# All down products of the first expert layer in three rounded passes, W2's split ahead of the layer, and the next layer's weights loaded into the place of their low parts

## The reference: what is computed

```python
x = x + cross_attention(layernorm(x), ctx)          # 16 heads of 8, 154 keys, masked
x = x + experts_0(layernorm(x))                     # 8 experts, 512 wide, top 2
x = x + second_attention(layernorm(x), ctx)         # causal, then cross, then a small feed-forward
x = x + experts_1(layernorm(x))                     # 32 experts, 64 wide, top 6 of 4 groups, a shared one
# experts_0:
h = gelu(einsum('td,edh->eth', xf, W1) + b1[:, None, :])
expert_out = einsum('eth,ehd->etd', h, W2) + b2[:, None, :]
out = einsum('etd,te->td', expert_out, weights)
```

## Time and profile before

| | us |
|---|---|
| median of three executions | 574.48 |
| lowest, highest | 572.86, 574.75 |
| profiled execution, its own time | 574.52 |
| its span, first to last instruction | 572.7 |
| PE busy | 556.3 (97%) |
| DVE busy | 447.4 (78%) |
| ACT busy | 376.1 (66%) |
| POOL busy | 170.1 (30%) |

### The profile page before, as it was taken

The page is one execution under the profiler, slowest core; times in us unless marked ns, Lnnn a source line. Parts: engine busy times, 40 slices in busy tenths (PEclk is TensorE's granted clock), DMA queues, the critical chain, the costliest instruction groups (busy, mean ns, idle before and its releaser), DMA issues.

```text
span 572.7 us, 8759 instructions
## 1 busy us (share of the span) xinstructions
PE 556.3 (97%) x2677; PEld 393.5 (69%) x2677; DVE 447.4 (78%) x1343; ACT 376.1 (66%) x663; POOL 170.1 (30%) x173
## 2 busy tenths in 40 slices
PE   7898999999999999999999999999999999999996
PEld 7565566665777667767677667677776766677885
DVE  6988999792555656877868787988988999879794
ACT  2576677768766787856976589873765532475553
POOL 4101120011242212163113324137012031455574
PEclk9999999999999999999999999999999999999998
DMA  4401000401111110111101111341221231432540
GB/s 137 186 19 29 1 9 2 148 1 38 56 38 38 38 47 19 38 38 40 69 31 37 58 36 38 106 147 57 92 92 68 99 98 64 146 110 84 158 146 24
DMA packets 23328, 38.42 MB, mean 67 GB/s; under 512 B 3792, under 2 KB 9552, under 8 KB 22896
## 3 DMA queue, kind: packets, MB, share of 16 engines
q1 hardware_dynamic: 22848, 37.44, 20.1%
q10 hardware_dynamic: 432, 0.40, 0.2%
HBM read 36.45 MB, written 1.38 MB: 66 GB/s over the span
## 4 chain that ended last, share of the span: by engine, by line
PE 86%; DVE 6%; ACT 3%; issue 2%; POOL 1%; DMA 1%; POOLq 0%; SPq 0%; ACTq 0%; DVEq 0%
PE ps L1640 11%; PE ps L1642 10%; PE ps L1641 10%; PE ps L1863 8%; PE ps L2036 5%; PE ps L1652 4%; PE ps L1739 4%; PE ps L1653 3%; PE ps L1654 3%; PE ps L1759 3%; PE ps L1635 3%; PE ps L1647 2%; PE ps L1773 2%; PE ps L1776 2%; PE ps L1940 2%
## 5 line engine op out<-in xcount | busy, mean ns | idle before, releaser
L1640 PE MATMUL ps<-xThi,w1s 128*128 128x512 f32 x256 | 122.5, 479 | 1.3 <-DVE h L1591 0.6
L999 ACT ACTIVATE h<-ps,early 128x512 f32<-128x512 f32 x128 | 86.1, 686 | 47.5 <-PE ps L1642 25.1
L1642 PE MATMUL ps<-xTlo,w1s 128*128 128x512 f32 x256 | 100.8, 394 | 0.0
L1641 PE MATMUL ps<-xThi,w1s 128*128 128x512 f32 x256 | 100.5, 393 | 0.0
L1130 ACT ACTIVATE s<-ps 128x512 f32<-128x512 f32 x68 | 40.7, 598 | 62.8 <-PE ps L1642 62.3
L862 POOL TENSOR_TENSOR acc_o<-acc_o,ty 128x512 f32<-128x512 f32 x32 | 43.6, 1361 | 85.1 <-DVE ty L1391 80.0
L1640 PEld LDWEIGHTS ps<-xThi,w1s 128*128 128x128 f32 x256 | 48.2, 188 | 26.3 <-issue 7.8
L1863 PE MATMUL ps<-h,w2s 128*128 128x512 f32 x128 | 65.8, 596 | 0.3 <-DVE ty L1391 0.3
L1295 DVE TENSOR_REDUCE NM<-ps 128x2 f32<-128x308 f32 x128 | 55.9, 471 | 5.5 <-PE ps L1739 3.8
L1352 DVE TENSOR_TENSOR h_r<-h,s_r 128x512 fp32r<-128x512 f32 x64 | 48.1, 752 | 14.7 <-ACT s_r L885 14.5
L1591 DVE TENSOR_TENSOR h<-s,ps 128x512 f32<-128x512 f32 x68 | 46.4, 682 | 15.7 <-PE ps L1642 12.0
(11 more groups left out here) (293 smaller groups left out, 1156.0 us busy)
## 6 DMA issues: line engine op xcount, KB each, us to landing
CB<-ct_rows SPq DMA_DIRECT2D x128, 128.0 KB, 2.9
WB<-wt_rows SPq DMA_DIRECT2D x32, 256.0 KB, 3.3
w2s<-w_dram SPq DMA_DIRECT2D x2, 2048.0 KB, 9.3
raw<-gu_dram SPq DMA_DIRECT2D x4, 512.0 KB, 4.1
x_in<-x_dram SPq DMA_DIRECT2D x4, 256.0 KB, 3.0
w2s<-dn_dram SPq DMA_DIRECT2D x1, 1024.0 KB, 4.7
out_dram<-ty SPq DMA_DIRECT2D x3, 256.0 KB, 3.0
late<-late_dram SPq DMA_DIRECT2D x1, 608.5 KB, 7.8
```

The costliest lines, as they stand in the source:

```text
L999: nc.scalar.activation(h32[:, c % HR, :], bank[c % 2], ACT.Gelu, bias=b1T[:, c:c + 1]).then_inc(b_gelu.sem, 1)
L1640: M(dst, w[0], xThi[:, x, :], start=start, stop=False)
L1641: M(dst, w[1], xThi[:, x, :], start=False, stop=False)
L1642: return M(dst, w[0], xTlo[:, x, :], start=False, stop=stop)
```

## The change

- `second`: every chunk's down product is `down3`; the f32 product of L1863 is gone.
- `highs_b` and `lows_b` run over all 32 chunks of a block instead of 16. The rounded copies rotate over three buffers (s32 and its twin hh0 have three slots instead of two) and no longer wait in pairs.
- `split2` has four pieces instead of two, contiguous ones; w2h holds all 4096 columns.
- The buffer raw1 is gone. A piece of the second layer's weights is loaded into the place of its low part (w1f and shf, the f32 twins of w1s and shs), and SP waits for PE's last reading of W1 there (`b_h_ps`) before the DMA. ACT then copies the high part, with no wait on PE, and POOL subtracts in place.
- All five tables of order are written anew.

```diff
-    w1s = sb("w1s", [P, 2, NC0 * P], F32R)
+    w1f, w1s = twins("w1s", [P, 2, NC0 * P])
-    w2h = sb("w2h", [P, NP1 * P], F32R)
-    odd, odd_low = (w.rearrange("p (c two k) -> p c two k", two=2, k=P)[:, :, 1, :] for w in (w2s[:], w2r[:]))
+    w2h = sb("w2h", [P, NC0 * P], F32R)
-    shs = sb("shs", [P, 2, 2 * P], F32R)
+    shf, shs = twins("shs", [P, 2, 2 * P])
-    s32, hh0 = twins("s32", [P, 2, S])
+    s32, hh0 = twins("s32", [P, 3, S])
+    HH = s32.shape[1]
-    raw1 = sb("raw1", [P, 2, 1024])
@@ SP, second_weights
-            for k, (src, w, _, _) in enumerate(pieces1):
-                yield
-                if not k:
-                    sp.wait_ge(a_x1.sem, a_x1.at(NB - 1, 1))
+            for k, (src, raw, _, _) in enumerate(pieces1):
+                yield
+                if k:
+                    sp.wait_ge(b_h_ps.sem, b_h_ps.at(NB - 1, 8 * k))
                 if k >= 2:
-                    sp.wait_ge(gu_lo.sem, k - 1)
-                sp.dma_start(raw1[:, k % 2, 0:w], src).then_inc(gu_loaded[k % 2].sem, 16)
+                    sp.wait_ge(gu_hi.sem, k - 1)
+                sp.dma_start(raw, src).then_inc(gu_loaded[k % 2].sem, 16)
@@ ACT, split1
-                if k:
-                    act.wait_ge(b_h_ps.sem, b_h_ps.at(NB - 1, 8 * k))
-                copy(dst[:, 0, c:c + w], raw1[:, k % 2, 0:w]).then_inc(gu_hi.sem, 1)
+                copy(hi, raw).then_inc(gu_hi.sem, 1)
@@ ACT, split2
-            for k in range(2):
+            for k in range(NDOWN):
                 yield
                 act.wait_ge(down0_loaded.sem, 16)
                 c = slice(1024 * k, 1024 * k + 1024)
-                copy(w2h[:, c].rearrange("p (c k) -> p c k", k=P), odd[:, 8 * k:8 * k + 8, :]).then_inc(w2_hi.sem, 1)
+                copy(w2h[:, c], w2s[:, c]).then_inc(w2_hi.sem, 1)
@@ ACT, highs_b
-            for j in range(NC0 // 2):
-                yield
-                act.wait_ge(b_gelu.sem, b_gelu.at(b, 2 * j + 2))
-                if b or j >= 2:
-                    act.wait_ge(b_y.sem, b_y.at(b, 2 * j - 2))
-                copy(hh0[:, j % 2, :], h32[:, (2 * j + 1) % HR, :]).then_inc(b_hi.sem, 1)
+            for c in range(NC0):
+                yield
+                act.wait_ge(b_gelu.sem, b_gelu.at(b, c + 1))
+                if b * NC0 + c >= HH:
+                    act.wait_ge(b_y.sem, b_y.at(b, c - HH + 1))
+                copy(hh0[:, (b * NC0 + c) % HH, :], h32[:, c % HR, :]).then_inc(b_hi.sem, 1)
@@ DVE, lows_b
-            for j in range(NC0 // 2):
+            for c in range(NC0):
                 yield
-                dve.wait_ge(b_hi.sem, b_hi.at(b, j + 1))
-                o = (2 * j + 1) % HR
-                V.tensor_tensor(h32r[:, o, :], h32[:, o, :], hh0[:, j % 2, :].bitcast(F32), ALU.subtract).then_inc(b_lo.sem, 1)
+                dve.wait_ge(b_hi.sem, b_hi.at(b, c + 1))
+                o = c % HR
+                V.tensor_tensor(h32r[:, o, :], h32[:, o, :], hh0[:, (b * NC0 + c) % HH, :].bitcast(F32), ALU.subtract).then_inc(b_lo.sem, 1)
@@ PE, second
-                j, at, ends = c // 2, c % 4 == 0, c % 4 == 3
-                if c % 2:
-                    pe.wait_ge(b_lo.sem, b_lo.at(b, j + 1))
-                    if b == 0 and j % 8 == 0:
-                        pe.wait_ge(w2_lo.sem, w2_lo.at(0, j // 8 + 1))
-                    w = w2h[:, j * P:(j + 1) * P], odd_low[:, j, :]
-                    down3(bank[2], w, (hh0[:, j % 2, :], h32r[:, c % HR, :]), at, ends).then_inc(b_y.sem, 1)
-                else:
-                    pe.wait_ge(b_gelu.sem, b_gelu.at(b, c + 1))
-                    M(bank[2], w2s[:, c * P:(c + 1) * P], h32[:, c % HR, :], start=at, stop=ends).then_inc(b_y.sem, 1)
+                at, ends, k = c % 4 == 0, c % 4 == 3, slice(c * P, (c + 1) * P)
+                pe.wait_ge(b_lo.sem, b_lo.at(b, c + 1))
+                if b == 0 and c % 8 == 0:
+                    pe.wait_ge(w2_lo.sem, w2_lo.at(0, c // 8 + 1))
+                down3(bank[2], (w2h[:, k], w2r[:, k]), (hh0[:, (b * NC0 + c) % HH, :], h32r[:, c % HR, :]), at, ends).then_inc(b_y.sem, 1)
...
 PLAN_ACT = {
-    "split2": [[12505, 14718]],
+    "split2": [[11383, 11522, 12013, 12100]],
```

More of the change, by code:

```diff
@@ L136 @@
[L136 to L144, removed]
@@ new lines @@
+    "halves_b": [[11478, 11945], [16472, 17004], [19960, 22069], [26317, 27260]],
+    "routing": [[11610, 11632, 11672, 12497, 12518, 12540, 12562, 12582], [16506, 16575, 17063, 17253, 18212, 18284,
+        18306, 18326], [20985, 21007, 21186, 21370, 22317, 22877, 22947, 23557], [27995, 28150, 28603, 28717, 29548,
+        30311, 30333, 30353]],
+    "stage_b": [[14234, 14884, 15491, 16181, 16712, 17271, 17910, 18393, 18674], [19495, 20444, 21127, 22003, 22758,
+        23679, 24236, 24767, 25050], [25934, 26578, 27725, 28619, 29256, 30000, 30593, 31402, 31771], [32308, 33559,
+        34237, 35274, 35869, 37028, 37737, 38183, 38650]],
@@ L310 @@
-    "prepare_b": [[10641, 11519, 12824], [15687, 17325, 18503], [19336, 21013, 23741], [27123, 27562, 31110]],
-    "first": [[12729, 13169, 13459, 13620, 13688, 13850, 13918, 14214, 14282, 14509, 14732, 14801, 15028, 15096, 15320,
[8 rows of a table removed]
-    "weights": [[13311], [19016], [25875], [32779]],
-    "second": [[13534, 13990, 14059, 14145, 14354, 14440, 14578, 14664, 14873, 14959, 15165, 15251, 15460, 15730,
[8 rows of a table removed]
-    "stage_c": [[16103, 17503, 19260, 19380, 19633, 19719], [25964, 26040, 26224, 26310], [32364, 32733, 32868, 32954]
-        , [38731, 39465, 39738, 39893]],
@@ L341 @@
[L341 to L342 removed]
[8 rows of a table removed]
[L351 removed]
[4 rows of a table removed]
+    "idle_turns": [[88, 156, 200, 245, 290, 335, 380, 424, 469, 514, 559, 604, 648, 688, 1138, 1213, 1236, 1258, 1333,
+        1356, 1442, 1740, 1980, 2097]],
@@ new lines @@
+    "context_keys": [[779], [1564], [4695], [7880]],
+    "context_values": [[720], [4263], [7264], [10126]],
+    "inputs": [[899, 1037], [2309, 2792], [5147, 5809], [8307, 8442]],
+    "queries": [[1387, 1683, 1891, 3090], [3811, 4743, 4987, 5991], [6826, 7710, 8073, 8914], [9498, 10530, 10805,
+        11675]],
+    "keys": [[1170, 1290], [3569, 3629], [6600, 6723], [9022, 10211]],
+    "maxima": [[1526, 1547, 1620, 1658, 1727, 1763, 1828, 1866], [1941, 1958, 2049, 2075, 2147, 2215, 2353, 2415],
[7 rows of a table added]
@@ new lines @@
+    "prepare_b": [[10687, 11178, 12884], [15543, 15796, 18370], [19031, 20303, 23632], [26163, 27025, 30576]],
+    "first": [[12767, 13230, 13505, 13582, 13673, 14008, 14077, 14307, 14447, 14516, 14722, 14860, 14929, 15141, 15334,
[8 rows of a table added]
+    "weights": [[13371], [18802], [25545], [32365]],
+    "second": [[13802, 13871, 13939, 14146, 14379, 14585, 14654, 14791, 15003, 15072, 15265, 15403, 15659, 15727,
[8 rows of a table added]
+    "stage_c": [[15222, 16229, 18657, 19212, 19397, 20712], [25400, 25634, 25818, 25904], [32229, 32307, 32454, 32541]
+        , [38345, 39278, 39465, 39731]],
@@ L657, in build_program @@
     NPIECE, NHALF = 4, 8
-    pieces1 = [(a["sh"][:, 0:2 * P], 2 * P, shs, 0)]
-    pieces1 += [(a["gu"][:, 1024 * k:1024 * k + 1024], 1024, gus, 1024 * k) for k in range(NPIECE)]
+    pieces1 = [(a["sh"][:, 0:2 * P], shf[:, 1, :], shs[:, 0, :], shs[:, 1, :])]
+    for k in range(NPIECE):
+        c = slice(1024 * k, 1024 * k + 1024)
+        pieces1.append((a["gu"][:, c], w1f[:, 1, c], gus[:, 0, c], gus[:, 1, c]))
     NZERO, NONE, NPAD, NLATE = 7, 2 + 2 + 2 * HG + 1, 3, 2
```

254 lines of the change are left out of this document (122 added, 132 removed), and 204 rows, old and new, of tables (PLAN_ACT, PLAN_DVE, PLAN_PE, PLAN_SP).

## The result

Two sets of executions, alternating on the same chip:

| | median us | lowest, highest | n |
|---|---|---|---|
| before | 574.3 | 572.86, 574.75 | 4 |
| changed | 578.39 | 578.29, 579.44 | 4 |

The account below looks back on a forecast made before the run. PE, busy in 97% of the span, was taken to bound the kernel, with DVE and ACT limiting the fourth block after the change. 574.5 - 3.2 (blocks) + 1.2 (chain start) = 572.5 us, range 569.3 to 576.8.

Parts of the forecast that it names:

- The new order: All engines' lists from the attention stage on: no row prices the reordering, allowance of 1 us either way.
- a change of more than 2 us ahead of the first gelu: Sign named beforehand that the forecast is wrong, in the stage ahead of the first expert layer's blocks.
- The sum, block by block: First expert layer's four blocks, bounded by PE, ACT or DVE: 243.6 us instead of 246.8, 3.2 us less.
- the start of the chain: First down product now waits for gelu, copy and low part: 1.2 us more, taken once.
- Filling of 95%: Share of a block that ACT's or DVE's in-order queue can fill, taken between 91% and 100%.
- My 91% case: Four blocks with queues filled to only 91%: 251.8 us, 5.0 more than before.
- PE's price: 64 f32 down products on PE become three passes, 0.69 instead of 0.85 us each: 10.2 us off PE.
- PE leads and the others follow: First expert layer before the change: ACT and DVE wait on PE with slack; PE's weight loads waited only 5.2 us.
- The load of ACT and DVE: Per block, 16 added copies at 0.54 us, 8.6 us on ACT; low parts at 0.66 us, 10.6 us on DVE.
- DVE decides: Rival: low parts cost 0.80 us beside POOL's additions, slowing third and fourth blocks: 577.1 us, chance 0.18.
- Nothing to be seen: Rival: DVE backlog slides into the second layer's first block and eats the gain: 574 us, chance 0.20.
- W2's split and the weights: Added W2 pieces fit gaps ahead of the first gelu; second layer's weights have some 29 us of cover: nothing.

Follow-up runs that it names:

- e5: The changed kernel with one row of POOL's table, the places of four constant memsets, as in the kernel before: 574.5 us, ratio 1.0008 to before.
- e6: The kernel before with the four memsets of POOL's constants placed late, as in the changed kernel: 576.79 us, ratio 1.0047 to before.
- e3: The changed kernel with low parts of even chunks left out on DVE, all rounded copies kept: 575.5 us, ratio 1.0031 to before.
- e1: The changed kernel's tables, weights' path and split, but even chunks are one f32 product again without copy or low part: 579.66 us, ratio 1.0103 to before.
- e2: The changed kernel, three passes for all chunks, but copies and low parts made for odd chunks only: 572.18 us, ratio 0.9959 to before.
- e12: The kernel before plus 64 spare copies on ACT and 64 spare subtractions on DVE, each ahead of a real one: 601.14 us, ratio 1.0492.
- e13: The kernel before plus 64 spare copies on ACT and 64 spare subtractions on DVE, each behind a real one: 598.36 us, ratio 1.043.
- e9: e5 with four s_r buffers for the rounded copies instead of three: 574.84 us, ratio 1.0023 to the kernel before.
- e10: e9 with five h32 buffers instead of four as well: 574.7 us, ratio 1.0022 to the kernel before.
- e11: e2's work under the tables of the kernel before, with W2's split in four pieces and the new weights' path: 572.0 us, ratio 0.9976 to before.
- e8: The changed kernel with POOL's 32 additions cut from 512 to 32 columns: 574.82 us, ratio 1.0018 to the kernel before.
- e14: e5 and e8 together, memsets at their old place and POOL's additions cut: 571.22 us, ratio 0.9962 to the kernel before.

## Why the prediction was wrong

- **The new order, "1 us either way is my allowance".** This is the step that put the time outside the range. One row of POOL's table, four moved memsets, cost 3.9 us of the 4.1 (e5), 2.8 in the kernel before (e6). I had named a change of more than 2 us ahead of the first gelu as a sign of being wrong and had the lists at hand, but looked only at the places of the layer. A list has to be read from its first row. With the memsets back the kernel is at 574.5: 2.0 over the forecast, in its range, and no change.
- **The sum, block by block: "3.2 us less".** This is the second step that failed, and it stays so with the memsets back. Forecast blocks 48.8, 62.7, 64.3, 67.8 and 1.2 for the start of the chain, in all 2.0 us less; measured 49.5, 64.3, 66.5, 70.7, 4.2 us more. With the 2.5 us less behind them, the layer and what follows are 1.7 us longer (1.6 in e5). Blocks one and two got shorter by 1.9 and 1.0 us, not by 2.6.
- **What makes up the miss.** The time was 5.9 us over the forecast: 3.9 us for the memsets, some 3.6 for the blocks and what follows, and less 1.6 ahead of the layer, where e5's first gelu is at 137.1 against 138.7. No term of mine gave that 1.6. It is luck, and without it the kernel with the memsets back would have been slower than before (an estimate: 574.5 + 1.6 us).
- **Filling of 95%.** The block sum let PE, ACT or DVE bound each block by its own busy time. In the fourth DVE is filled to 65.50 / 70.70 = 93%, which looks like the bound that I forecast. It is not: with DVE at 79% the fourth block took 70.8 us (e3), with the old work under the new lists 69.5 (e1), and with neither link added 68.0 (e2). In the second and third DVE is filled to 84% and 86%. My 91% case gave 251.8 us for the four blocks and 251.0 were measured, but that is luck, since it had DVE at 91% of the third. The two links cost 6.2 us in this order (e2 against after), and the bare load, with no other engine waiting for it, 24.5 to 28 us in the order of before (e12, e13). A quotient of busy time and length prices neither. What bounds these blocks is not shown. More buffers bring nothing (e9, e10), so it is not the depth of the rings. Whether it is the load or the longer chain that costs under the new lists stays open.
- **PE's price, 64 x (0.85 - 0.69) = 10.2 us.** The price stands by the starts in the timeline, though PE's busy time fell by 7.9 us only. Under one order it gave 7.4 us (e1 to e2); under the old tables 3.7 us in the blocks (e11). "PE leads and the others follow" was true of the waits before; with cheaper products PE stood idle for part of what it gained, even with no link added (4.8 us in e11).
- **The load of ACT and DVE.** Sizes were right: 0.54 and 0.66 us gave 219.9 us of DVE in four blocks, measured 213.2, and ACT 222.5 against 216.0. The stretch of a low part was underrated a little: 0.771 us on the mean instead of 0.745.
- **The rival "DVE decides".** Forecast 577.1 for a price of 0.80 us; the time was near it by luck, for other reasons in the main. Its mechanism is real in part: without most of POOL's additions 3.6 us go (e8), and 3.3 with the memsets back (e14 against e5). How much of that the kernel before already paid was not measured.
- **"Nothing to be seen".** With the memsets back this is where the kernel stands, though not by a backlog of DVE: behind the blocks it got shorter by 2.5 us, not longer.
- **W2's split and the weights: nothing.** Not contradicted in the changed kernel: no DMA wait of note shows before the second layer's gates, and e5's first gelu is early with all four pieces ahead of it. Under the old tables (e11) the first gelu is 2.7 us late with the two more pieces put in; the forecast's 2.1 us for uncovered pieces is near that, but no run tests them alone.
- **Open.** What bounds the second to fourth block, and how much of the remaining loss a better fitted list could win. Nor is it shown which instructions of the fourth block came out of the second layer, or why the attention stage of e5 is 1.6 us shorter.

## What to carry to other kernels

Where engines run fixed lists, read the new list of every engine from its first row, and look above all for instructions of GpSimd that slide beside VectorE's first work: here nothing in the stage that the edit was about showed them. Work taken from the busiest engine and given to two others comes back only in part. Here 7.4 of 10.2 us came back with nothing added in return, and the two added links took 6.2 away again, with neither of the other engines full. Measure it by the same work in the same order with one link left out. An order fits one load: with work added whose results nobody waits for, next to each real copy and low part, the lists of before lost 25 us.

## What the hardware did that I had not expected

POOL's memsets, which read no SBUF, held up small DVE instructions with one input each, of 0.16 to 0.19 us, for 2.7 to 3.1 us: two of them in the changed kernel, three in e6, none in e5. They started beside the memset of 2.23 us and ended only behind a later one that followed it without a gap: 0.03 to 0.04 us behind the third in the changed kernel, 0.05 to 0.07 behind the fourth in e6. A tensor_tensor of DVE with two SBUF inputs that started at 7.01, beside the same memset, took its usual 0.16 us.

The Trainium skill, page "SBUF — State Buffer", section "Who interferes with whom", lists cast and tensor_scalar among VectorE operations that can enter a mode with both port pairs, and says that whoever issues first gets the shared pair and the other "fully blocks". The rows agree for a GpSimd instruction that only writes; that the held instructions ran in that mode no view shows. Of the low parts, which have two SBUF inputs, the section says that they contend with GpSimd instructions that read, and not with those that only write: the pair at 340 us agrees, the low part ending 0.55 us behind the addition, and so does the tensor_tensor at 7.01.

After 3.39 us of idle TensorE at the start of its work, the granted clock had a mean of 0.76 over 7.1 us, in the changed kernel and in e6 (idle for 3.44 us) alike, and 1.00 in e5 (idle for 0.72). The stall of 2.5 us (11.48 against 8.96 for the first transposes) was 4.1 us at the first exponential. The 3.4 us at half the clock would account for 1.7 us, about the difference; this is an estimate.
